# A conv, router and expert matmul kernel: slot buffers laid over the first expert's landing area, later weights over the row buffers, slot loads moved to SyncE, experts ordered fullest first

## What is computed

```python
y = conv_general_dilated(x, w, padding=[(K - 1, 0)], feature_group_count=D) + b
logits = einsum('bsh,eh->bse', y, w_router)
idx = argmax(logits, axis=-1)
all_out = einsum('bsh,efh->bsef', y, w_experts)
out = x + take_along_axis(all_out, idx[:, :, None, None], axis=2)[:, :, 0, :]
```

## Time and profile before

| | |
|---|---|
| median of 3 runs | 547.17 us (546.49 to 550.29) |
| profiled execution, device time | 548.22 us |
| its span | 546.3 us |
| TensorE busy | 508.5 us (93%) |
| VectorE / ScalarE / GpSimd busy | 284.5 / 149.1 / 132.1 us |
| mean granted TensorE clock | 0.972 |
| moved by DMA | 130.28 MB, 238 GB/s over the span |
| 1680 expert matmuls (35 slots) | 386.7 us busy |
| 1024 conv matmuls | 121.2 us busy |

### The profile page before, as it was taken

How to read it: one execution, slowest core, us unless ns; L and a number is a source line. 1 busy time by engine, 2 the same in 40 slices (tenths; PEclk the granted TensorE clock), 3 DMA queues, 4 the chain that set the end, 5 groups by cost and what they waited for, 6 DMA issues and landing times.

```text
span 546.3 us, 9011 instructions
## 1 busy us (share of the span) xinstructions
PE 508.5 (93%) x2740; PEld 439.2 (80%) x2741; DVE 284.5 (52%) x369; ACT 149.1 (27%) x255; POOL 132.1 (24%) x148
## 2 busy tenths in 40 slices
PE   5999999696299999999699999999999999999995
PEld 5999999696288787888488888888888888888884
DVE  5854473345765523429748432277227722475581
ACT  2443434254200101115525100061006100151430
POOL 1004132060243013321122131210322032121323
PEclk9999999799599999999799999999999999999998
DMA  8958979996646895668999765459646965579635
GB/s 314 401 155 260 352 228 365 245 316 263 176 195 232 273 308 149 188 197 298 314 283 364 244 174 172 122 201 360 187 130 192 347 179 165 155 241 295 192 120 187
DMA packets 59187, 130.28 MB, mean 238 GB/s; under 512 B 12704, under 2 KB 32416, under 8 KB 59168
## 3 DMA queue, kind: packets, MB, share of 16 engines
q1 hardware_dynamic: 19392, 58.22, 32.6%
q0 software_dynamic: 14832, 54.27, 28.2%
q10 hardware_dynamic: 24944, 17.55, 13.4%
HBM read 94.56 MB, written 35.45 MB: 238 GB/s over the span
## 4 chain that ended last, share of the span: by engine, by line
PE 59%; issue 3%; DMA 2%; DVE 1%; ACTq 1%; ACT 0%; POOL 0%; DVEq 0%; POOLq 0%
PE ps L747 59%; DMA x_row<-x_rows,idx 2%; DVE w_sb L591 1%; ACT w_sb L377 0%; ACTq L271 0%; DVE x_row L613 0%; DMA out<-x_row,idx 0%; ACTq L393 0%; DVE ys L605 0%; DVE y_cols L600 0%; POOL out L815 0%; DVEq L616 0%; ACTq L391 0%; ACTq L273 0%; ACTq L380 0%
## 5 line engine op out<-in xcount | busy, mean ns | idle before, releaser
L747 PE MATMUL ps<-w_sb,ys 128*128 128x512 f32 x1680 | 386.7, 393 | 19.7 <-issue 13.1
L747 PEld LDWEIGHTS ps<-w_sb,ys 128*128 128x128 f32 x1680 | 318.2, 190 | 87.5 <-issue 15.5
L705 PE MATMUL ps<-mats,xs 128*128 128x128 f32 x1024 | 121.2, 283 | 7.6 <-DMA xs<-x_both 5.8
L705 PEld LDWEIGHTS ps<-mats,xs 128*128 128x128 f32 x1024 | 119.9, 199 | 7.8 <-DVE mats L440 5.4
L600 DVE STREAM_TRANSPOSE y_cols<-y_blk 128x1024 f32<-128x1024 f32 x36 | 44.8, 1244 | 146.5 <-PE ps L747 121.1
L386 ACT CAST ys<-y_cols 128x1024 fp32r<-128x1024 f32 x36 | 37.9, 1053 | 276.4 <-DVE y_cols L600 260.4
L591 DVE TENSOR_TENSOR w_sb<-w_raw,w_sb 128x1024 fp32r<-128x1024 f32 x64 | 73.9, 1219 | 26.5 <-ACT w_sb L377 26.4
L377 ACT CAST w_sb<-w_raw 128x1024 fp32r<-128x1024 f32 x64 | 62.2, 1045 | 28.3 <-issue 16.9
L815 POOL DMA_INDIRECT out<-x_row,idx x35 | 40.8, 1164 | 94.9 <-DVE x_row L613 90.1
L803 POOL DMA_INDIRECT y_sorted<-rows,pos_i x32 | 35.0, 1093 | 102.2 <-PE ps L705 64.1
L822 POOL COPY idx<-ids_all 128x1 int32 (+1 forms) x36 | 12.0, 335 | 178.9 <-DMA out<-x_row,idx 139.1
(11 more groups left out here) (88 smaller groups left out, 33.9 us busy)
## 6 DMA issues: line engine op xcount, KB each, us to landing
w_raw<-experts SPq DMA_DIRECT2D x64, 512.0 KB, 7.6
y_blk<-y_sorted ACTq DMA_DIRECT2D x132, 128.0 KB, 3.7
xs<-x_t SPq DMA_DIRECT2D x48, 256.0 KB, 5.9
xs<-x_both SPq DMA_DIRECT2D x16, 512.0 KB, 7.9
y_blk<-y_sorted SPq DMA_DIRECT2D x20, 128.0 KB, 2.7
x_row<-x_rows,idx POOLq DMA_INDIRECT x36, 4.7
out<-x_row,idx POOLq DMA_INDIRECT x35, 4.8
ids_all<-y_sorted ACTq DMA_DIRECT2D x33, 1.0 KB, 4.5
```

The lines of the kernel that those rows point to most:

```text
L705: mm = nc.tensor.matmul(to, xs[:, n % X_RING, s % PACK, :], mats[:, s, :].rearrange("p (u n) -> p u n", n=SIDE), start=(s == sets[0]), sto ...
L747: mm = nc.tensor.matmul(out_ps[k][:, f * HALF:(f + 1) * HALF], ys[k][:, a, c, :], w_sb[:, c, b, f * HALF:(f + 1) * HALF], start=(c == 0 an ...
```

## The change

- **Memory.** The landing area of the first expert is now `w_first`, and the slot buffers lie over it: `y_blk` over chunks 0 and 1, `y_cols` over 2 and 3, `ys[0]` over 4 and 5, `x_row` over 6 and 7. Later experts have two landing areas, `w_raw[0]` over `rows[0]` and `w_raw[1]` over `rows[1]`.
- **Waits that follow from it.** The loads of slots 0 and 1 wait for the split of chunk 0 and 1 and stand between the last loads of x (after packs 60 and 62 of 0 to 63). `turn_blocks(0)` and `(1)` wait for the split of chunks 2 and 3, `high_y(0)` for that of chunk 5, and the first gathers for that of all eight. The first gathers and slots 0 and 1 wait no more for group 2's scatter; slot 2 does.
- **Later weights.** Both following experts are loaded at once when the table is known, before slot 5 is loaded. When an expert is split, the one after the next is loaded into its area (`replace_raw`).
- **Slot loads.** SyncE issues all of them, and ScalarE none. Slots 3 and 4 wait for a new signal, `rows_ready`, that comes when the table's rows are known, ahead of the rest of it.
- **Order of experts.** Behind the lead's slots the experts come by the number of their slots, fullest first. This adds steps to `slot_starts`.
- **VectorE's order in the groups.** `choose` of the group before comes after three packs are doubled, not five.
- **Start.** The first pack of x, its factors and its matrices come in two halves, and the constants are loaded after the first pack.

```diff
-        w_raw = sb("w_raw", [P, HC, H])
+        w_first = sb("w_first", [P, HC, H])
-        y_blk = over("y_blk", [P, RING, 4, HC, PIECE], rows_at)
-        y_cols = [over(f"y_cols{k}", [P, HC, P], rows_at + (8 + 4 * k) * KB) for k in range(RING)]
-        x_row = over("x_row", [P, RING, H], rows_at + 16 * KB)
+        w_raw = [over(f"w_raw{k}", [P, HC, H], rows_at + k * row_bytes) for k in range(2)]
+        y_blk = over("y_blk", [P, RING, 4, HC, PIECE], raw_at)
+        y_cols = [over(f"y_cols{k}", [P, HC, P], raw_at + (8 + 4 * k) * KB) for k in range(RING)]
+        x_row = over("x_row", [P, RING, H], raw_at + 24 * KB)
...
+            def replace_raw(t, loads):
+
+                new = sp.value_load(tab_i[0:1, 2, bass.ds(t, 1)], min_val=0, max_val=2)
+                for k in range(2):
+                    with sp.If(new == k + 1):
+                        nth = sp.value_load(tab_i[0:1, 1, bass.ds(t, 1)], min_val=1, max_val=EXPERTS - 1)
+                        with sp.If(nth < loads - 1):
+                            e = sp.value_load(load_i[0:1, bass.ds(nth + 1, 1)], min_val=0, max_val=EXPERTS - 1)
+                            for c in range(HC):
+
+                                sp.wait_ge(w_split, nth * HC + (c + 1))
+                                sp.dma_start(w_raw[k][:, c, :], chunk(e, c)).then_inc(raw_in[k][c], 16)
...
             load_factors(0)
-            load_x(sp, 0)
+            x_0 = xs[:, 0, :, :].rearrange("p c t -> p (c t)")
+            sp.dma_start(x_0[:, 0:START_SETS * P], x_both[0][:, 0:START_SETS * P]).then_inc(x_start, 16)
+            sp.dma_start(x_0[:, START_SETS * P:], x_both[0][:, START_SETS * P:]).then_inc(x_in[0], 16)
+            load_factors(1)
...
-            sp.wait_ge(y_out[0], 2 * TPG * 16)
-            sp.wait_ge(y_out[1], TPG * 16)
-            for t in range(RING):
-                load_y(sp, lead_row(t), t, ids_all[:, t:t + 1, :])
+                if n in Y_AFTER:
+                    t = Y_AFTER.index(n)
+
+                    sp.wait_ge(y_out[t], TPG * 16)
+                    sp.wait_ge(w_split, t + 1)
+                    load_y(sp, lead_row(t), t, ids_all[:, t:t + 1, :])
...
-            sp.wait_ge(table_ready, 1)
+            sp.wait_ge(rows_ready, 1)
             sp.wait_ge(y_out[1], 2 * TPG * 16)
             for t in range(FIRST, FIRST + RING):
...
+            sp.wait_ge(table_ready, 1)
             loads = sp.value_load(one_i[0:1, 1:2], min_val=0, max_val=EXPERTS - 1)
-            with sp.Fori(0, EXPERTS - 1) as n:
-                with sp.If(n < loads):
-                    e = sp.value_load(load_i[0:1, bass.ds(n, 1)], min_val=0, max_val=EXPERTS - 1)
+            for k in range(2):
+                with sp.If(k < loads):
+                    e = sp.value_load(load_i[0:1, k:k + 1], min_val=0, max_val=EXPERTS - 1)
                     for c in range(HC):
-
-                        sp.wait_ge(w_split, n * HC + (c + 1))
-                        load_raw(e, c)
+                        sp.dma_start(w_raw[k][:, c, :], chunk(e, c)).then_inc(raw_in[k][c], 16)
+
+            sp.wait_ge(y_blocks, FIRST + 1)
+            load_slot(FIRST + 2, (FIRST + 2) % RING)
+            replace_raw(FIRST, loads)
+            last = sp.value_load(one_i[0:1, 3:4], min_val=0, max_val=ROUNDS - 1)
+            with sp.Fori(0, ROUNDS) as i:
+                with sp.If(i < last + 1):
+                    for k in range(RING):
+                        t = i * RING + (FIRST + k)
+
+                        sp.wait_ge(y_blocks, t + 2)
+                        load_slot(t + 3, (FIRST + k + 1) % RING)
+                        replace_raw(t + 1, loads)
...
                 if b == BANKS - 1:
+
+                    act.wait_ge(w_split, 6)
                     high_y(0, 0)
...
                         high_y(t + 1, (FIRST + k + 1) % RING)
-                        load_slot(t + 3, (FIRST + k + 1) % RING)
                         high_w(t + 1)
...
-                for k in range(5):
+                for k in range(3):
                     double(n + k)
                 choose(g - 1)
-                double(n + 5)
-                double(n + 6)
+                for k in range(3, 7):
+                    double(n + k)
                 place_rows(g - 1)
...
-            low(0, 4)
+            low(0, 4, w_first)
+
+            dve.wait_ge(w_split, 3)
             turn_blocks(0, 0, 1)
-            low(0, 5)
+            low(0, 5, w_first)
+
+            dve.wait_ge(w_split, 4)
             turn_blocks(1, 1, 1)
             sum_most(LAST)
-            low(0, 6)
+            low(0, 6, w_first)
             low_y(0, 0)
...
-            pool.wait_ge(y_out[0], 2 * TPG * 16)
+            pool.wait_ge(w_split, HC)
             for t in range(RING):
                 look_up(t, t, 1, t + 1)
```

More of the change, by code:

```diff
@@ L80 @@
 C_SPLIT = C_NTH + EXPERTS
[L81 removed]
+C_ZERO = C_SPLIT + TILES
+C_SLOT = C_ZERO + EXPERTS
 C_TOKEN = C_SLOT + SLOTS
@@ L248, in build @@
         third_known = sem("third_known")
+        rows_ready = sem("rows_ready")
         table_ready = sem("table_ready")
-        raw_in = [sem(f"raw_in{c}") for c in range(HC)]
+        first_in = [sem(f"first_in{c}") for c in range(HC)]
+        raw_in = [[sem(f"raw_in{k}_{c}") for c in range(HC)] for k in range(2)]
         w_hi = sem("w_hi")
@@ L389, in high_w @@
             def high_w(t):
-                new = act.value_load(tab_i[0:1, 2, bass.ds(t, 1)], min_val=0, max_val=1)
-                with act.If(new == 1):
-                    nth = act.value_load(tab_i[0:1, 1, bass.ds(t, 1)], min_val=1, max_val=EXPERTS - 1)
-                    for c in range(HC):
-                        act.wait_ge(gemm_chunk, (t - 1) * HC + (c + 1))
-                        high(nth, c)
+                new = act.value_load(tab_i[0:1, 2, bass.ds(t, 1)], min_val=0, max_val=2)
+                for k in range(2):
+                    with act.If(new == k + 1):
+                        nth = act.value_load(tab_i[0:1, 1, bass.ds(t, 1)], min_val=1, max_val=EXPERTS - 1)
+                        for c in range(HC):
+                            act.wait_ge(gemm_chunk, (t - 1) * HC + (c + 1))
+                            high(c, w_raw[k], raw_in[k][c], nth * 8 + 8 * (1 - k))
             for g in range(LAST):
@@ L409, in _ @@
                     act.wait_ge(conv_mm, sets_done(LAST, 2 * PACK * (ready[0] + 1)))
-                    high(0, ready.pop(0))
+                    c = ready.pop(0)
+                    high(c, w_first, first_in[c], 16)
             high_y(1, 1)
@@ L498, in place_rows @@
                 step(V.tensor_copy(base, place[:, TPG, :]))
-            count, lead, others, rest, start, n_of, flag, more, nth, tmp, tail, done = (per[:, i, :] for i in range(1, 13))
+            count, lead, others, rest, start, n_of, flag, more, nth, tmp, tail, done, sign = (per[:, i, :] for i in range(1, 14))
             full_row = one[:, 5:6]
@@ L545, in slot_starts @@
                 step(V.scalar_tensor_tensor(out=flag, in0=n_of, scalar=0.0, in1=others, op0=ALU.is_gt, op1=ALU.mult))
-                step(V.tensor_tensor_scan(more, const(C_ONES), flag, 0.0, ALU.mult, ALU.add))
-                step(V.tensor_tensor(nth, more, others, ALU.mult))
+                step(V.tensor_reduce(one[:, 7:8], flag, AX.X, ALU.add))
+                step(V.tensor_copy(load_i[:, 0:EXPERTS], nth))
+                step(V.tensor_scalar(load_i[:, 0:EXPERTS], load_i[:, 0:EXPERTS], 1, None, ALU.bitwise_and))
+                step(V.tensor_copy(sign, load_i[:, 0:EXPERTS]))
+                step(V.scalar_tensor_tensor(out=sign, in0=sign, scalar=1.0, in1=flag, op0=ALU.add, op1=ALU.mult))
+                step(V.tensor_scalar(nth, nth, 1.0, None, ALU.add))
+                step(V.tensor_tensor(nth, nth, flag, ALU.mult))
                 step(V.tensor_scalar(tail, count, -float(P), 0.0, ALU.add, ALU.max))
@@ L585, in slot_table, with low @@
                 step(V.tensor_scalar(one_i[:, 3:4], one_i[:, 7:8], RING.bit_length() - 1, None, ALU.logical_shift_right))
-                V.tensor_copy(one_i[:, 1:2], more[:, EXPERTS - 1:EXPERTS]).then_inc(table_ready, 1)
-            def low(n, c):
+                V.tensor_copy(one_i[:, 1:2], one[:, 7:8]).then_inc(table_ready, 1)
+            def low(n, c, raw):
                 dve.wait_ge(w_hi, n * HC + (c + 1))
-                V.tensor_tensor(w_sb[:, c, LO, :], w_raw[:, c, :], w_sb[:, c, HI, :].bitcast(F32), ALU.subtract
+                V.tensor_tensor(w_sb[:, c, LO, :], raw[:, c, :], w_sb[:, c, HI, :].bitcast(F32), ALU.subtract
                                 ).then_inc(w_split, 1)
@@ L615, in low_w @@
             def low_w(t):
-                new = dve.value_load(tab_i[0:1, 2, bass.ds(t, 1)], min_val=0, max_val=1)
-                with dve.If(new == 1):
-                    nth_load = dve.value_load(tab_i[0:1, 1, bass.ds(t, 1)], min_val=1, max_val=EXPERTS - 1)
-                    for c in range(HC):
-                        low(nth_load, c)
```

(11 more changed lines are left out.)

88 lines of the change are left out of this document (52 added, 36 removed).

## The result

The changed kernel takes 553.5 us (median of 4 runs, 550.67 to 557.13) against 546.93 us (546.49 to 550.29) for the kernel before: a ratio of 1.0113, 95% interval 1.0075 to 1.0150. It is slower, by 1.1%. I had forecast 544.1 us in a range of 531 to 551.

What follows compares the result with a forecast made beforehand. TensorE's timeline was taken to bound the kernel: first expert matmul at 139.7, 390.4 us behind it and a 13.1 us new stall make a span of 543.2; 0.9 added gives 544.1 us, range 531 to 551.

Steps and rivals of the forecast that it cites:

- The transition: Between convolution and first expert matmul: earlier row loads bring that matmul from 146.66 to 139.7 us, between 138 and 142.3.
- 2.6 us at 410 GB/s, 4.3 at 248: Delay of pack 63 in group 3 from 1.06 MB of rows of slots 0 and 1 put ahead of it.
- pack 63 is late: Rival at the end of group 3: SyncE's waits and extra rows end doublings at 136 or more; 548.9 us, chance 0.12.
- E: End of VectorE's doublings in group 3, forecast at 131.4 us, bounds 129.7 and 134.
- The burst: Sixteen weight loads for two experts ahead of slot 5's rows on one queue: a stall before slot 5, costing 13.1 us.
- G': New start of the first expert matmul, forecast at 139.7 us, between 138 and 142.3; before it was 146.66.
- S: New stall before slot 5: 10.5 us of waiting plus 2.6 of low clock, 13.1 us.
- Short experts: Later slots: fullest-first order and weights two experts ahead remove the single-slot expert's 5.16 us gap and 2.6 of slow clock.
- The gaps before slots 3 and 5 of the earlier trace: TensorE's gaps of 0.96 and 0.47 us before these slots, counted as a gain of 1.4 us.
- Choose earlier: Group 3: removes TensorE's 4.30 us gap before the rank but gains nothing, as landing of x bounds the doubling.
- The start: First pack of x in halves, constants later: all up to 100 us moves forward 1.2 us, between 0 and 2.
- Sum: Whole kernel: 139.7 + 390.4 + 13.1 = 543.2 us of span, before 546.3; 544.1 us with 0.9 added.

Runs made afterwards that it cites:

- e13: Changed kernel with weights loaded a second time in 4 KB packets where the rows of slots 0 and 1 stood, those rows behind x: 552.19 us, ratio 1.0099.
- e10: Changed kernel with SyncE's waits for the split of chunks 0 and 1 kept, but the rows of slots 0 and 1 behind all x: 548.93 us, ratio 1.0043.
- e1: Changed kernel with only one later expert loaded ahead of slot 5, the second behind slot 6's rows: 538.99 us, ratio 0.9846.
- e4: Changed kernel with all sixteen weight loads kept, but the rows of slots 5 and later issued from ScalarE's queue: 540.51 us, ratio 0.9874.
- e6: Changed kernel with rows of slots 0 and 1 behind x, one later expert ahead of slot 5, and later experts ordered by index: 536.64 us, ratio 0.9810.
- e5: Changed kernel with rows of slots 0 and 1 behind x, one later expert ahead of slot 5, and choose after five packs: 534.13 us, ratio 0.9753.
- e7: Changed kernel with rows of slots 0 and 1 behind x, one later expert ahead of slot 5, and the old start: 533.79 us, ratio 0.9754.
- e9: Changed kernel with slots 0 and 1 behind x, one later expert ahead of slot 5, VectorE's sum and low parts before slot 0's turn: 532.02 us, ratio 0.9725.
- e12: Changed kernel with the rows of slots 0 and 1 issued by ScalarE between its casts of group 3, none on SyncE: 548.29 us, ratio 1.0006.

## Why the prediction was wrong, point by point

- **The transition: the step that failed.** I put the end of the doublings at 131.4, bounds 129.7 and 134; it was 139.2, and the first matmul at 147.2 instead of 139.7. The working behind it held: from there to the first matmul it took 8.1 us where I had 8.3. Of the 7.8 us, 4.8 are the term that was mis-sized, what the rows cost x: "2.6 us at 410 GB/s, 4.3 at 248". From pack 57's doubling to the end I had 14.4 us, 11.3 as before and 3.1 for the rows; it took 19.2. Counted from pack 60, in three traces, the rows cost 7.7 to 8.1 us. 410 is the rate of all queues together. While group 2's scatter ran on GpSimd's queue, SyncE's, with the rows in pieces of 1 KB, moved 82 GB/s of 408 (0.49 MB from 124 to 130 us), and 190 with large packets (e13), which cost 5.2 us.
- **The transition, the rest.** The other 3.0 us of the 7.8 were there at pack 57 already, doubled at 120.0 where I had 117.0: 1.2 are the gain of the start, which did not come, and 1.8 lie within what differs between traces (117.1 to 120.8). I also timed only pack 63, which SyncE issues last. Pack 61 was the one that came late: its place in the ring was free at about 108, and it stood behind the wait, the rows and their issue; by e10 the wait did no harm. The rival "pack 63 is late" had the right kind of cause, and E at 136 as its size; I gave it 0.12.
- **The burst: right, and the size nearly so.** Predicted: slot 5 at G' + 67.9 and S = 13.1. Measured: 216.94 - 147.24 = 69.7, and 14.7. The burst began at G' + 30.8 (31.5 forecast). The mean rate from 178 to 213.1 us was 335 GB/s, under my 350 and just over the 329 of the earlier trace rows. That it came near is partly luck, since it is made of 400 while weights and large packets passed and 213 at the end, which I had not foreseen. e1 and e4 show the cause.
- **Short experts: right.** No gap at a change of expert. The order, which I counted with it, is hardly needed: the areas and ScalarE's freedom do it (e6).
- **The gaps before slots 3 and 5 of the earlier trace rows.** The one before slot 3 closed, as predicted.
- **Choose earlier: right** at nothing (e5). The 4.30 us gap went and came back as waits of 0.4 to 1.8 us for x, and the granted clock stayed at 2.4 GHz (1.00 in 94 to 118, 0.86 before), which brought nothing either.
- **The start: wrong by 1.2 us.** The first matmul came at 4.10, but 0.99 and two smaller waits for packs 1 to 3 followed, and group 0's end moved by 0.3 us (rank 0 at 42.04). e7 measures no gain. I had counted bytes ahead of pack 0 and not of the packs behind it.
- **Sum.** 543.2 us of span forecast, 552.3 measured: 7.5 us from all ahead of the first expert matmul (4.8 of them the rows) and 1.6 from the burst.

The mechanism that makes the kernel slower is therefore the one priced, a burst ahead of slot 5, on top of a transition that gained nothing. Without the burst it would be faster (e1, 0.985); with the transition mended too, 0.978, and 0.9725 in e9.

## What to carry to other kernels

A load that is wanted soon must not stand behind loads wanted late in one engine's DMA queue: move it ahead, or issue it from another engine, where it shares instead of queueing (e4, e12). Price such a queue by the part of the rate that it gets beside others, not by the rate of all DMA: here a queue with small packets beside one with large ones kept level in packets and fell behind in bytes. And when a gap is bound by landings (share 1.03), taking away an earlier wait of the engine gives nothing back.
